# Expert rows of a top-2 mixture added to one row per token in HBM by an accumulating scatter, in place of a scatter, a reload and sums on the engines

## The reference

```python
x = L0_attn_x
x = x + 0.5 * ffn(layernorm(x))      # pass 0
x = x + attention(layernorm(x))      # one head of 128, per batch, Wo and bo behind it
x = x + 0.5 * ffn(layernorm(x))      # pass 1, the same weights

def ffn(x):                          # 8 experts, TOP_K = 2
    logits = x @ W_gate + b_gate
    _, top_idx = top_k(logits, 2)
    y_all = relu(einsum('bsd,edh->bseh', x, W_e) + b_e)
    return take_along_axis(y_all, top_idx[..., None], axis=2).mean(axis=2)
```

## Time and profile before

| what | value |
|---|---|
| median of three runs | 309.33 us (308.43 to 310.49) |
| span of the profiled execution | 309.0 us |
| PE busy / DVE / POOL / ACT | 258.0 / 180.9 / 147.6 / 98.5 us |
| granted TensorE clock, mean | 0.908 of full speed |
| DMA | 47.24 MB, mean 153 GB/s |
| `scatter` (line 442) | 46 instructions, mean 1017 ns of POOL |
| `gather` (line 434) | 46 instructions, mean 1010 ns of POOL |

### The profile page before, as it was taken

How to read it: one execution, slowest core, us unless ns; L and a number is a source line. 1 busy time by engine, 2 the same in 40 slices (tenths; PEclk the granted TensorE clock), 3 DMA queues, 4 the chain that set the end, 5 groups by cost and what they waited for, 6 DMA issues and landing times. The chain is left out here.

```text
span 309.0 us, 4801 instructions
## 1 busy us (share of the span) xinstructions
PE 258.0 (84%) x1271; PEld 184.7 (60%) x1272; DVE 180.9 (59%) x379; ACT 98.5 (32%) x177; POOL 147.6 (48%) x150
## 2 busy tenths in 40 slices
PE   7948674899999999994999998838999999999400
PEld 2314222378888888853878684413888888888300
DVE  4995989733444434367688837884344344443691
ACT  0652642324233342411234533221232433324100
POOL 4570653735666656334856400005356666563450
PEclk9975855799999999997999999996999999999955
DMA  6995641384453434526230101213354444345792
GB/s 243 378 405 200 225 137 48 97 267 158 158 169 126 148 127 161 178 68 185 78 136 0 70 15 55 83 55 97 105 147 151 167 132 159 116 159 200 286 319 108
DMA packets 22434, 47.24 MB, mean 153 GB/s; under 512 B 4237, under 2 KB 4877, under 8 KB 22417
## 3 DMA queue, kind: packets, MB, share of 16 engines
q1 hardware_dynamic: 12208, 22.35, 20.9%
q0 software_dynamic: 7360, 20.46, 20.8%
q10 hardware_dynamic: 2850, 4.23, 3.7%
HBM read 32.34 MB, written 18.35 MB: 164 GB/s over the span
## 5 line engine op out<-in xcount | busy, mean ns | idle before, releaser
L442 POOL DMA_INDIRECT z_dram<-yrow,place x46 | 46.8, 1017 | 58.3 <-ACT yrow L568 50.0
L1093 DVE TENSOR_TENSOR xt_lo<-tp_ps,xt_hi 128x512 fp32r<-128x512 f32 x46 | 31.8, 692 | 57.7 <-ACT xt_hi L561 57.1
L434 POOL DMA_INDIRECT xg<-xn_dram,tok x46 | 46.5, 1010 | 32.3 <-DVE tok L1080 17.5
L568 ACT ACTIVATE yrow<-ypre 128x512 f32<-128x512 f32 x46 | 29.1, 633 | 99.0 <-issue 50.6
L561 ACT ACTIVATE xt_hi<-tp_ps 128x512 fp32r<-128x512 f32 x46 | 26.8, 582 | 11.9 <-PE tp_ps L741 11.9
L741 PE MATMUL tp_ps<-ident,xg 128*128 128x128 f32 x184 | 27.9, 274 | 1.5 <-DMA xg<-xn_dram,tok 0.8
L427 POOL TENSOR_TENSOR rstd<-var_eps,neg_half 128x2 f32<-128x2 f32 x12 | 9.4, 787 | 40.6 <-DVE var_eps L946 38.4
L1101 DVE TENSOR_TENSOR ypre<-y_ps,be_bc 128x512 f32<-128x512 f32 x24 | 16.6, 692 | 20.8 <-PE y_ps L756 20.8
L756 PE MATMUL y_ps<-whi,xt_hi 128*128 x96 | 27.9, 413 | 0.6 <-issue 0.6
L741 PEld LDWEIGHTS tp_ps<-ident,xg 128*128 128x128 f32 x184 | 22.7, 141 | 9.1 <-issue 1.8
L694 PE MATMUL g_ps<-xt_gate,wg 128*8 128x256 f32 x64 | 20.2, 472 | 9.2 <-DVE topi L968 9.0
(11 more groups left out here) (135 smaller groups left out, 407.9 us busy)
## 6 DMA issues: line engine op xcount, KB each, us to landing
raw<-in_L_ffn_W_e_dram SPq DMA_DIRECT2D x16, 512.0 KB, 6.8
z_rows<-z_dram SPq DMA_DIRECT2D x8, 512.0 KB, 3.6
xn_dram<-xn ACTq DMA_DIRECT2D x12, 256.0 KB, 2.2
x<-in_L_attn_x_dram SPq DMA_DIRECT2D x4, 512.0 KB, 5.5
z_last<-z_dram SPq DMA_DIRECT2D x4, 512.0 KB, 6.1
out_dram<-x SPq DMA_DIRECT2D x8, 256.0 KB, 3.8
xn_dram<-xn_more ACTq DMA_DIRECT2D x4, 256.0 KB, 3.5
z_rows<-z_dram SPq DMA_DIRECT2D x4, 256.0 KB, 2.8
```

The source lines that it names most:

```text
L434: pool.indirect_dma_start(out=xg[:, t % XG, :], out_offset=None, in_=xn_dram[f][:, :], in_offset=bass.IndirectOffsetOnAxis(ap=tok[:, t:t + ...
L442: pool.indirect_dma_start(out=z_dram[f][:, :], out_offset=bass.IndirectOffsetOnAxis(ap=place[:, t:t + 1], axis=0), in_=yrow[:, t % YB, :], ...
L568: act.activation(yrow[:, t % YB, :], ypre[:, t % 2, :], ACT.Relu, scale=HALF_MEAN).then_inc(yrow_made, 1)
L1093: dve.tensor_tensor(xt_lo[:, t % 2, :], tp_ps[(n0 + t) % 2][:], xt_hi[:, t % 2, :].bitcast(F32), ALU.subtract).then_inc(xt_made, 1)
```

## The change

There is one row per token now: `acc_dram[f]` with T + 128 rows, the last 128 being spare. It begins as x, the scatter adds to it in the DMA (`compute_op=ALU.add`), and it is read back as the new x, or copied to the output. Rows without a pair add to the spare row T + p. As two tiles can hold the two pairs of one token, each scatter waits until the one before it has landed. One semaphore, `added`, counts the scatters of both passes.

```diff
 (SP, behind the loads of the experts' weights)
+            sp.dma_start(acc_dram[0][0:T, :], x_rows).then_inc(acc_begun[0], 16)
+            sp.dma_start(acc_dram[0][T:T + P, :], x_rows[0:P, :]).then_inc(acc_begun[0], 16)
+            sp.dma_start(acc_dram[1][T:T + P, :], x_rows[0:P, :]).then_inc(acc_begun[1], 16)
...
 (SP; wait_scatters, load_z, the stores of x and their waits are removed)
+            def wait_added(f):
+                sp.wait_ge(sent_made, f + 1)
+                sp.wait_ge(added, sp.value_load(sent[0:1, 0:1], min_val=16 * (f * NS + 1),
+                                                max_val=16 * (f + 1) * NS))
+            wait_added(0)
             for i in range(NT):
+                sp.dma_start(x[:, i, :], acc_dram[0][i * P:(i + 1) * P, :]).then_inc(x_ffn[i], 16)
+            for i in range(NT):
+                sp.wait_ge(x_att, i + 1)
+                sp.dma_start(acc_dram[1][i * P:(i + 1) * P, :], x[:, i, :]).then_inc(acc_begun[1], 16)
+            wait_added(1)
+            for b in range(B):
+                sp.dma_start(out_rows[b * S:(b + 1) * S, :], acc_dram[1][b * S:(b + 1) * S, :]
+                             ).then_inc(out_stored, 16)
+            sp.wait_ge(added, 16 * 2 * NS)
+            sp.wait_ge(out_stored, 16 * B)
...
 (POOL)
             def scatter(f, t):
                 pool.wait_ge(yrow_made, f * NS + t + 1)
+                if t:
+                    pool.wait_ge(added, 16 * (f * NS + t))
                 pool.indirect_dma_start(
-                    out=z_dram[f][:, :], out_offset=bass.IndirectOffsetOnAxis(ap=place[:, t:t + 1], axis=0),
-                    in_=yrow[:, t % YB, :], in_offset=None, bounds_check=TOP_K * T - 1, oob_is_err=False
-                ).then_inc(scattered[t % YB], 16)
+                    out=acc_dram[f][:, :], out_offset=bass.IndirectOffsetOnAxis(ap=dest[:, t:t + 1], axis=0),
+                    in_=yrow[:, t % YB, :], in_offset=None, bounds_check=T + P - 1, oob_is_err=True,
+                    compute_op=ALU.add).then_inc(added, 16)
...
                 for t in range(XG + 1):
                     gather(f, t)
+                pool.wait_ge(dest_made, f + 1)
+                pool.wait_ge(acc_begun[f], 16 * (2, NT + 1)[f])
...
-            def sum_z(f, i):                   (and all its calls)
...
 (ACT)
-                        act.wait_ge(scattered[t % YB], sent)
+                        act.wait_ge(added, sent)      (16 * (f * NS + t - 2): tile t - 3 has landed)
...
-                    for s in range(YB):
-                        act.wait_ge(scattered[s], 16 * slot_uses(YB, s))
+                    act.wait_ge(added, 16 * NS)
...
 (PE)
-            pe.wait_ge(z_first[0][0], 16)
+            pe.wait_ge(x_ffn[0], 16)
...
 (DVE)
-                    if (kind, b) == ("att", 0):
-                        add_z(0, i)
-                        dve.wait_ge(x_ffn, i + 1)
+                    if kind == "att":
+                        dve.wait_ge(x_ffn[TB * b + i], 16)
...
             def count_sent(f):                 (one instruction in place of three or four)
+                dve.tensor_scalar(sent[:], incl[0:1, E - 1:E], 16.0, 16.0 * f * NS, ALU.mult, ALU.add
+                                  ).then_inc(sent_made, 1)
+            def destinations():                (called behind the instruction that makes tok)
+                dve.tensor_scalar(dest[:], place[:], spare_row[:], None, ALU.min).then_inc(dest_made, 1)
...
-            def add_z(f, i):                   (add_z_batch too, and all their calls)
...
-            for s in range(YB):
-                dve.wait_ge(scattered[s], 16 * slot_uses(YB, s))
+            dve.wait_ge(added, 16 * NS)
             add_bv(0)
```

More of the change, by code:

```diff
@@ L64, in macaron_kernel @@
         xn_dram = [nc.dram_tensor(f"xn_dram{f}", [T, H], F32, kind="Internal") for f in range(2)]
-        z_dram = [nc.dram_tensor(f"z_dram{f}", [TOP_K * T, H], F32, kind="Internal") for f in range(2)]
+        acc_dram = [nc.dram_tensor(f"acc_dram{f}", [T + P, H], F32, kind="Internal") for f in range(2)]
         XN = 4
@@ L78, in macaron_kernel @@
         be_bc = sb("be_bc", [P, E * H])
-        with ExitStack() as end:
-            z_mid = sb("z_mid", [P, 2, TOP_K, H], at=end)
         wqkv = sb("wqkv", [P, NC, 3 * D])
@@ L104, in macaron_kernel @@
         part_id = sb("part_id", [P, 1])
+        spare_row = sb("spare_row", [P, 1])
         place_id = sb("place_id", [P, J])
@@ L117, in macaron_kernel @@
         place = sb("place", [P, NS], U32)
+        dest = sb("dest", [P, NS], U32)
         tok = sb("tok", [P, NS], U32)
@@ L120, in macaron_kernel @@
         eid = sb("eid", [1, NS], I32)
[L121 to L125, removed]
+        sent = sb("sent", [1, 1], I32)
         nmax = sb("nmax", [P, TB])
@@ L153, in macaron_kernel @@
                 ot = prob[:, 0, :]
-                z_rows = sb("z_rows", [P, ZB, TOP_K, H], at=part)
         with ExitStack() as shared:
@@ L188, in macaron_kernel @@
         PE_CONSTS = 3
-        CONSTS = 12 + YB
+        CONSTS = 12
         ATT_LOADS = 5
@@ L230, in macaron_kernel @@
         yrow_made = sem("yrow_made")
[L231 to L235, removed]
+        dest_made = sem("dest_made")
+        acc_begun = [sem(f"acc_begun{f}") for f in range(2)]
+        added = sem("added")
+        x_ffn = [sem(f"x_ffn{i}") for i in range(NT)]
         bo_added = sem("bo_added")
@@ L339, in _ @@
             sp.dma_start(bo_bc[:], b_o.partition_broadcast(P)).then_inc(att_in, 16)
-            def wait_scatters(f):
+            def wait_added(f):
                 sp.wait_ge(sent_made, f + 1)
-                counts = [sp.value_load(sent[0:1, s:s + 1], min_val=16 * (T * TOP_K // P // YB),
-                                        max_val=16 * 2 * NS) for s in range(YB)]
-                for s in range(YB):
[L348 to L367, removed]
@@ L412, in _ @@
             pool.memset(zeros_e[:], 0.0).then_inc(const_made, 1)
[L413 to L416, removed]
             pool.wait_ge(const_made, CONSTS)
@@ L456, in experts @@
                     scatter(f, t)
[L458 to L465, removed]
             def add_bo(b):
@@ L470, in add_bo @@
                     pool.tensor_tensor(x[:, i, :], x[:, i, :], bo_bc[:], ALU.add).then_inc(bo_added, 1)
[L472 to L475, removed]
             for b in range(B):
@@ L483, in _ @@
             deviations("att", 0)
-            attention_input(1)
+            deviations("att", 1)
             add_bo(0)
@@ L487, in _ @@
             for b in range(B):
-                if b + 2 < B:
-                    for i in range(TB * (b + 2), TB * (b + 3)):
-                        sum_z(0, i)
                 if b:
@@ L497, in _ @@
             experts(1)
-            for i in SUM_END:
-                sum_z(1, i)
         @block.scalar
@@ L566, in relu @@
                     if sent is not None:
-                        act.wait_ge(scattered[t % YB], sent)
+                        act.wait_ge(added, sent)
                     act.activation(yrow[:, t % YB, :], ypre[:, t % 2, :], ACT.Relu,
@@ L585, in experts @@
                         hi_rows(t + 1, r * STEP + (n0 + t + 2), r * STEP + (f * NS + t))
-                        relu(t, r * STEP + (f * NS + t + 1), r * (16 * STEP // YB) + sent(t))
+                        relu(t, r * STEP + (f * NS + t + 1), r * (16 * STEP) + sent(t))
                 for t in range(REST, NS):
@@ L1030, in count_sent, with destinations @@
             def count_sent(f):
[L1033 to L1041, removed]
+                dve.tensor_scalar(sent[:], incl[0:1, E - 1:E], 16.0, 16.0 * f * NS, ALU.mult, ALU.add
+                                  ).then_inc(sent_made, 1)
+            def destinations():
+                dve.tensor_scalar(dest[:], place[:], spare_row[:], None, ALU.min).then_inc(dest_made, 1)
             def route(f, halves_left):
@@ L1080, in route @@
                 dve.tensor_single_scalar(tok[:], place[:], T - 1, ALU.bitwise_and).then_inc(tok_made, 1)
+                destinations()
                 if f:
@@ L1119, in experts @@
                     tile(t)
[L1121 to L1128, removed]
-                    done.then_inc(x_ffn, 1)
-                elif f == 0 or i in SUM_END:
-                    dve.wait_ge(z_summed, NT - TB + SUM_END.index(i) + 1 if f else i - TB + 1)
-                    dve.tensor_tensor(x[:, i, :], x[:, i, :], z_slot(f, i)[:, 0, :], ALU.add
-                                      ).then_inc(x_ffn, 1)
-                else:
-                    dve.wait_ge(z_in[1][i], 16)
-                    link(dve.tensor_tensor(x[:, i, :], x[:, i, :], z_slot(1, i)[:, 0, :], ALU.add))
-                    dve.tensor_tensor(x[:, i, :], x[:, i, :], z_slot(1, i)[:, 1, :], ALU.add
-                                      ).then_inc(x_ffn, 1)
-            def add_z_batch(b):
-                for i in range(TB * b, TB * (b + 1)):
-                    add_z(0, i)
-                dve.wait_ge(x_ffn, TB * (b + 1))
```

(2 more changed lines are left out.)

27 lines of the change are left out of this document (5 added, 22 removed).

## The result

The kernel after takes 418.73 us (median of four runs, 417.37 to 420.49), the kernel before 309.61 us in the same comparison (308.43 to 310.49). The ratio is 1.351, with a 95% interval from 1.346 to 1.356: slower by 35%. The profiled execution has a span of 418.7 us, 109.7 us over the one before.

What follows compares the result with a forecast made beforehand. PE bounds the kernel at 3.21 us a tile; the waiting scatter's loop, 0.78 + 1.01 + 3.11 = 4.90 us, replaces it. 45 C - 155.4 = +65.1 us on 309.0 gives 374 us, range 328 to 425.

Steps and rivals of the forecast that it cites:

- What bounds the kernel: Both passes before the change: PE alone sets the pace, 3.21 us a tile; scatters follow it, none waiting for another.
- Wake: POOL, from the end of a scatter's wait to its descriptors: 0.78 us, expected to stay after the new wait.
- Descriptors: POOL's descriptor time per adding scatter: taken as 1.01 us, as for the plain one, bounds 1.01 and 2.02.
- Landing: From a scatter's descriptors to its landing: 3.11 us, as 1.72 plain, 0.57 for reading HBM, 0.82 for the second 256 KB.
- The sum: Whole kernel: change of 45 C - 155.4 = +65.1 us on 309.0, so 374; chance 0.40 for 356 to 392.
- C: Period of the waiting scatters in both passes, wake plus descriptors plus landing: 4.90 us against 3.18 before.
- The eight loads of x ... lie in that: End of pass 0: loads issued four C (19.6 us) ahead of the last landing, so covered and adding nothing.
- The attention: Stage between the passes: POOL's sums, DVE's adds and their waits go; taken as 0, bounds -3 and +3 us.
- The tail: Work after pass 1: loads, sums and stores go, a gain of 10.3 us were C still 3.18.
- Quick landing: Rival for the scatter loop: landing quick as a plain one or wake hidden, 298 to 312 us, chance 0.09.
- The clock: Rival for PE in the passes: gaps lower its clock to 1.2 GHz, some 400 us, 432 at worst, chance 0.09.
- The expensive add: Rival for the scatter: landing 4.01 us gives 414 us, with doubled descriptors about 460; chance 0.20.

Runs made afterwards that it cites:

- The plain runs: Kernel after with a plain scatter that still waits: 330.5 us; kernel after with two rows per token, plain scatter and no wait: 309.2 us, ratio 0.998.
- the held-back copies: Kernel after, with SP's loads of x and copies to the output started only when all 23 scatters of the pass have landed: 422.3 us.
- the run with dropped rows: Kernel after, with rows without a pair dropped by the bounds check instead of added to spare rows: 398.4 us.

## Why the prediction was right in kind and short in size

*What bounds the kernel.* Right: PE's pace in both passes. With the wait, the scatter's loop took its place, as POOL's timeline and the chain show; the plain scatter with the wait had a period of 3.60 us, near the 3.51 that the rows of before gave.

*Wake.* Taken as 0.78, measured 0.87 from a landing to the next start, 0.75 of it "issue": 4 us over 45 periods. About right in size. Its explanation, that the gap is the MOVE's road, fell all but 0.10 us with the run without a bounds check.

*Descriptors.* This is the step that failed, the term with more than half of the 44.6 us by which the forecast was short. "I take 1.01, the row of the same instruction": it measured 1.59, inside the bounds of 1.01 and 2.02 but 0.58 off, and it counts 45 times, so 26 us. The plain runs put it down to the adding.

*Landing.* Taken as 3.11, measured 3.24: 6 us over 45 periods. The parts were nearly right too: I had 1.39 us over the plain landing for reading the old rows, the runs show 1.52, almost all of it time on the DMA engines (1.40) and not latency (0.57 in my sum).

*The sum.* C was 4.90, and is 5.7 over most tiles. The sum's own rule, 45 C - 155.4, gives +101 us with 5.7, where it gave +65.1.

*What lay beside.* "The eight loads of x ... lie in that", and the four copies to the output: they are covered in time, but they are not free. They hold up tile 19's scatter by 2.8 us in pass 0 and 4.8 us in pass 1, and every later scatter waits for that one. This term was put at nothing; the held-back copies showed it. With these 7.6 us, the first scatter 1.7 us earlier and the middle 1.2 us longer, the sum comes to +108, against 109.7. The last 1.6 us are single longer periods, the longest 6.63.

*The attention.* Right at about nothing: +1.2 us for the removal of all sums and adds.

*The tail.* The gain that the change has, 10.3 us by the sum, is real (8.4 from the plain run without the wait), and it is hidden behind some 110 us of waiting (45 times the 2.5 us between 5.7 and 3.2).

*Rivals.* Quick landing: no. Beside it stood a figure of the Trainium skill (DMA: Bandwidth & Descriptors, Anatomy of one DMA), by whose fit 256 KB take an estimated 2.6 us from issue to landing. The runs agree for the plain scatter (2.73) and not for the adding one (4.83). The Trainium skill's rule of two source reads (Collectives: The Full Stack, section on why ReduceScatter is half of AllGather), which it states of ReduceScatter, counts too little here: an adding 256 KB takes 2.2 us of the engines, 2.7 times a plain one. The clock: the forecast's sign was 1.00, and it did fall, to 0.90 over the passes. But a PE that is idle for a quarter of the time had the room, and the chain of pass 1 holds no PE between the scatters, so it cost nothing that can be seen. (The 0.44 us in the rival's price is a row at 209.59, where the clock was 0.50 too, not one of 40 to 50.) The expensive add, chance 0.20, is the nearest to what came: 414 was its time, though by a landing of 4.01 and descriptors of 1.01, where 3.24 and 1.59 were measured: that its time is so near is chance.

The time of 418.73 us lies in the range of 328 to 425, near its upper end; 374 was 45 us short. That it lies inside is in part luck: the upper end stood for doubled descriptors and a fallen clock at its worst, and what came was 0.58 of the 1.01 us of the first, nothing from the second, and the copies, which no bound of the range covered.

## What to carry to other kernels

Before an operation is put behind its own completion, work out the loop it makes (wake, issue, landing) and set it against the pace that it has to keep: here 3.5 us by the plain scatter's rows alone, against 3.21. An error of half a microsecond in such a loop counts as often as the loop turns, so the bounds of each term are worth more than the middle. An accumulating scatter is cheap where every row it touches is its own (some 2 us a pass here), and dear where order has to be bought with a wait; then also other transfers that seem covered lengthen the chain.

## What the runs showed of the hardware that was not expected

- An adding scatter of 128 rows of 2 KB takes POOL 1.59 us of descriptors, a plain one 1.01.
- It lands in 1.17 us without data, 2.2 us with 128 KB and 3.24 us with 256 KB added; a plain one with 256 KB in 1.72.
- POOL starts a scatter 0.87 us after the landing that held it, 0.77 us without the bounds check, and 0.30 us after the instruction before it when the wait is already met. A gather started 0.27 to 0.30 us after either, in the trace of before. Nothing here says why.
- An empty adding scatter that began 0.8 us behind the copies to the output landed 7.80 us after its issue began (in the run with dropped rows, DMA share 0.77 from 374 to 382), against 2.72 with the engines free: other transfers hold up even a completion that has no data.
